# Layer norms moved into the attention passes, a four-bank score ring in the last group, and router logits with the router as weights

## The reference

```python
def attn(c, Wq, Wk, Wv):                     # 16 heads of 16
    Q, K, V = (c @ W reshaped to heads)
    alpha = softmax(Q K^T / sqrt(16))        # over all 1024 keys
    alpha = where(causal, alpha, 0)          # masked after the softmax
    return alpha V
def ffn(x, router_w, w_fc, w_proj):          # 8 experts, hidden 1024
    probs = softmax(x @ router_w)            # top 2, weights made to sum to 1
    return sum_e combine[e] * (gelu(x @ w_fc[e]) @ w_proj[e])
x = x + layernorm(attn(layernorm(x)))
x = x + layernorm(ffn(layernorm(x)))
```

## Time and profile before

| | us |
|---|---|
| median of 3 runs (1714.86 to 1717.33) | 1716.28 |
| time of the profiled execution | 1713.16 |
| its span, as the trace has it | 1711.4 |
| PE busy | 1520.0 (89%) |
| DVE busy | 970.5 (57%) |
| ACT busy | 813.6 (48%) |
| POOL busy | 607.4 (35%) |

### The profile page before, as it was taken

The page is one execution under the profiler, slowest core; times in us unless marked ns, Lnnn a source line. Parts: engine busy times, 40 slices in busy tenths (PEclk is TensorE's granted clock), DMA queues, the critical chain, the costliest instruction groups (busy, mean ns, idle before and its releaser), DMA issues.

```text
span 1711.4 us, 30057 instructions
## 1 busy us (share of the span) xinstructions
PE 1520.0 (89%) x8598; PEld 762.7 (45%) x8599; DVE 970.5 (57%) x1716; ACT 813.6 (48%) x1713; POOL 607.4 (35%) x700
## 2 busy tenths in 40 slices
PE   5988999998999899899999854599999999999990
PEld 3541333333333333233333333366767767667660
DVE  5769777777777677777777776422222222222224
ACT  2330777776777677677777720222222222222224
POOL 5332434344434344343444320033333333333322
PEclk9995999999999999999999975699999999999995
DMA  3579022220222211222202142622122122122129
GB/s 123 178 167 258 1 38 38 38 39 2 38 38 38 39 22 17 39 38 38 39 1 84 65 179 68 206 34 37 31 31 36 31 33 34 31 35 33 31 28 200
DMA packets 87631, 105.09 MB, mean 61 GB/s; under 512 B 11648, under 2 KB 70912, under 8 KB 87520
## 3 DMA queue, kind: packets, MB, share of 16 engines
q1 hardware_dynamic: 69664, 80.80, 20.1%
q0 software_dynamic: 17856, 22.89, 8.5%
HBM read 64.70 MB, written 38.96 MB: 61 GB/s over the span
## 4 chain that ended last, share of the span: by engine, by line
PE 70%; issue 11%; DVE 7%; ACT 5%; POOL 4%; DMA 1%; SPq 0%; DVEq 0%; POOLq 0%; ACTq 0%
PE ps L1059 14%; PE ps L1079 14%; PE ps L934 12%; PE ps L906 10%; PE ps L999 9%; PE ps L1069 4%; ACT wfc L799 3%; DVE negmax L1321 3%; PE ps L899 2%; POOL x L616 2%; PE ps L954 1%; PE ps L1050 1%; PE ps L986 1%; ACT wfc L840 1%; PE ps L946 1%
## 5 line engine op out<-in xcount | busy, mean ns | idle before, releaser
L1321 DVE TENSOR_REDUCE negmax<-ps 128x1 f32<-128x1024 f32 x512 | 603.0, 1219 | 167.3 <-PE ps L999 164.5
L799 ACT ACTIVATE wfc<-ps 128x512 f32<-128x512 f32 x768 | 436.7, 595 | 181.2 <-PE ps L906 172.2
L1059 PE MATMUL ps<-wfc,yx 128*128 x568 | 257.5, 596 | 1.3 <-DVE yx L1433 0.7
L1079 PE MATMUL ps<-arena,yx 128*128 x1136 | 257.0, 379 | 0.4 <-ACT yx L824 0.4
L677 POOL TENSOR_TENSOR wfc<-wfc,causal 128x512 f32<-128x512 f32 x128 | 163.1, 1274 | 252.9 <-ACT wfc L799 203.3
L699 POOL DMA_INDIRECT expert_out<-yx,rt x71 | 112.6, 1586 | 366.2 <-DVE yx L1446 366.2
L999 PE MATMUL ps<-arena 96*128 96x512 bf16 x704 | 231.4, 413 | 9.4 <-DVE negmax L1321 4.1
L906 PE MATMUL ps<-arena 120*128 120x512 bf16 x528 | 206.4, 395 | 17.9 <-ACT wfc L799 4.2
L1079 PEld LDWEIGHTS ps<-arena,yx 128*128 128x128 f32 x1136 | 210.4, 190 | 26.8 <-issue 1.1
L821 ACT ACTIVATE yx<-ps 128x512 f32<-128x512 f32 x142 | 84.8, 597 | 206.0 <-PE ps L1059 206.0
L934 PE MATMUL ps<-wfc 128*16 128x128 f32 (+4 forms) x2304 | 161.8, 383 | 0.0
(11 more groups left out here) (169 smaller groups left out, 1491.3 us busy)
## 6 DMA issues: line engine op xcount, KB each, us to landing
arena<-qk_parts SPq DMA_DIRECT2D x132, 128.0 KB, 5.6
qk_parts<-x SPq DMA_DIRECT2D x32, 384.0 KB, 2.6
arena<-in_L_ffn_w_proj SPq DMA_DIRECT2D x8, 1024.0 KB, 10.6
wfc<-in_L_ffn_w_fc SPq DMA_DIRECT2D x16, 512.0 KB, 7.4
wfc<-qk_parts SPq DMA_DIRECT2D x60, 128.0 KB, 6.2
expert_out<-rt SPq DMA_DIRECT2D x3, 1408.0 KB, 13.1
yx<-in_L_attn_content SPq DMA_DIRECT2D x8, 512.0 KB, 3.9
x<-in_L_attn_content SPq DMA_DIRECT2D x1, 4096.0 KB, 25.2
```

Source lines behind the costliest of these rows:

```text
L799: nc.scalar.activation(et_sb[b % NET][:, hl, :], bk(ebank(c)), ACT.Exp).then_inc(s_expB, 1)
L1059: ins = nc.tensor.matmul(bk(1 + hf), xsT[:, kc, :], wfc[:, ds(off + (kc * FF + hf * 512), 512)], start=(kc == 0), stop=(kc == KC - 1))
L1079: ins = nc.tensor.matmul(bk(5 + s)[:, 0:D], hidT[:, c, :], arena[:, ds(off + c * D, D)], start=(c == 0), stop=(c == FC - 1))
L1321: nc.vector.tensor_reduce(negmax[:, hl % 2, i:i + 1], ps[:, 2 * (k % 2):2 * (k % 2) + 2, :], AX.XY, ALU.max, negate=True).then_inc(s_max, 1)
```

## The change

- Six passes (0 to 5) are written out and passes 6 to 14 are a loop of three turns.
- In each of passes 6 to 15 DVE does both norms of two tiles, one step after the maximum of a slot (`STEADY`), with POOL's roots in slots 10 and 21. These are tiles 0 to 19. Tiles 20 to 31 stay in groups of four (`FOURS`), two in the drain and one after it.
- The last group's chunks go through banks 4, 5, 1 and 2 and wait for the chunk four before.
- The router takes the eight groups in the order 0 to 5, 7, 6, six of them in the drain, one every six slots. Transposes and copies go through bank 0 one after the other. The logits are 8 matmuls of 128 columns with the router as weights (padded to 32 columns), in four column strips; ACT copies them (`copy_l`) and one matmul with the identity turns them back (`turn_back`) into bank 3, which DVE clears.
- `lo1` moves into `yx`, over rows that SP has stored: `place(i)` waits for the store of its group. `w_proj` 6 and 7 are loaded before attention ends, 4 and 5 after the permutation and after the first two gathers.

```diff
@@ ring and plan @@
-        def ebank(c):
+        LAST_RING = (4, 5, 1, 2)
+        def ebank(c, g):
+            if isinstance(g, int) and g == NGR - 1:
+                return LAST_RING[c % 4]
             return 4 + c % 2
...
-        LN_STEP, TAIL_END = 8, 49
-        at_stats = [LN_STEP * g + 1 for g in range(G)]
...
+        ORDER = (0, 1, 2, 3, 4, 5, 7, 6)
+        FIRST_LN, NPAIR = 6, NGR - 6
+        FOURS = (5, 7, 6)
+        IN_TAIL = 6
+        STEADY = {7: ("bn_y", 0), 8: ("bn_y", 1), 9: ("var_y", 0), 13: ("add", 0), 17: ("add", 1),
+                  18: ("bn_x", 0), 19: ("bn_x", 1), 20: ("var_x", 0), 24: ("scale", 0), 26: ("scale", 1)}
+        ROOT_Y, ROOT_X = 10, 21
+        at_bn_y, at_var_y, at_root_y, at_add = (0, 38), (1, 39), (1, 39), (3, 41)
+        at_bn_x, at_var_x, at_root_x, at_scale = (4, 42), (5, 44), (5, 44), (7, 46)
+        at_first = [1 + 6 * i for i in range(IN_TAIL)]
+        at_turn_x = [x + 2 * kc for x in at_first for kc in range(KC)]
+        at_logits = [x + 4 for x in at_first]
+        at_copy_l = [x + 5 for x in at_first]
+        at_back = [x + 6 for x in at_first]
+        at_choose = [x + 8 for x in at_first]
+        at_count = [x + 10 for x in at_first]
+        at_place = [x + 11 for x in at_first]
...
-            for p in range(NSL):
-                body(p, p)
-            with eng.Fori(0, (NGR - 1 - NSL) // NSL) as r:
+            for p in range(2 * NSL):
+                body(p, p % NSL)
+            with eng.Fori(0, (NGR - 1 - 2 * NSL) // NSL) as r:
@@ SP @@
+            for i in range(4):
+                store_x2(i)
             sp.wait_ge(s_ST, NCH * (NGR - 2))
+            for e in (6, 7):
+                load_wproj(e)
             sp.wait_ge(s_vc, NGR)
             for e in range(4):
                 load_wproj(e)
+            store_x2(4)
             sp.wait_ge(s_ST, NCH * (NGR - 1))
             for c in range(6 * KC, 8 * KC):
                 load_wfc(c)
+            store_x2(5)
             sp.wait_ge(s_pv, NBU * NGR)
             for c in range(4 * KC):
                 load_wfc(c)
             sp.wait_ge(s_T4, 2 * NGR)
             for c in range(4 * KC, 6 * KC):
                 load_wfc(c)
+            for i in range(6):
+                store_gate(i)
+            for i in range(6, G):
+                store_x2(i)
+            for i in range(6, G):
+                store_gate(i)
             sp.wait_ge(s_inv, NPR // PCE)
-            for e in range(4, E):
+            for s in range(2):
+                sp.wait_ge(s_xs[s], 16)
+            for e in (4, 5):
                 load_wproj(e)
@@ POOL @@
+                    if ln_live(p) and k == ROOT_Y:
+                        root_y(p - FIRST_LN, 2)
+                    if ln_live(p) and k == ROOT_X:
+                        root_x(p - FIRST_LN, 2)
@@ ACT @@
+            def copy_x2(i, kc):
+                act.wait_ge(s_x2t, KC * i + kc + 1)
+                nc.scalar.copy(x2T[:, kc, :], bk(x_bank(i, kc))).then_inc(s_x2e, 1)
+            def copy_l(i):
...
+                act.wait_ge(s_lt, i + 1)
+                nc.scalar.copy(lgT[:, :], bk(0)[:, 0:P]).then_inc(s_lc, 1)
@@ PE @@
-                wait_pos(pe, s_expB, NCH * g + c - 1)
+                if isinstance(g, int) and g == NGR - 1 and c >= 2:
+                    pe.wait_ge(*((s_max, QT * NH) if c < 4 else (s_expB, NCH * g + c - 3)))
+                else:
+                    wait_pos(pe, s_expB, NCH * g + c - 1)
...
-                        ins = nc.tensor.matmul(bk(2)[:, (g * TPC + t) * E:(g * TPC + t + 1) * E],
-                                               x2T[:, kc, t * P:(t + 1) * P], router[:, kc, :],
-                                               start=(kc == 0), stop=(kc == KC - 1))
+                        ins = nc.tensor.matmul(bk(0)[32 * t:32 * t + 32, 0:P], router[:, kc, :], x2T[:, kc, t * P:(t + 1) * P],
+                                               start=(kc == 0), stop=(kc == KC - 1), skip_group_check=True)
+                ins.then_inc(s_lt, 1)
+            def turn_back(i):
...
+                if i:
+                    pe.wait_ge(s_rp, CRP * (i - 1) + 1)
+                pe.wait_ge(s_lc, i + 1)
+                nc.tensor.matmul(bk(bank)[:, c0:c0 + TE], lgT[:, :], ...
@@ DVE @@
+                dve.wait_ge(s_x2w[i], 16)
                 dve.wait_ge(s_lo, 3 * i + 3)
                 for j in range(TOPK):
-                    ins = nc.vector.tensor_tensor(lo1[:, j, tiles, :], ...
+                    ins = nc.vector.tensor_tensor(lo1[:, g, j, :, :], ...
...
+                    if isinstance(p, int) and p == NGR and k == 0:
+                        dve.wait_ge(s_max, QT * NH)
+                        nc.vector.memset(bk(3), 0.0).then_inc(s_bz, 1)
...
+                    if ln_live(p) and k in STEADY:
+                        steady(p, k)
...
+            dve.wait_ge(s_const, NCONST)
             groups(dve, body)
-            for g in range(in_tail(at_stats), G + 2):
-                if g <= G:
-                    ln_first(g)
-                ln_second(g)
+            four_bn_y(2)
+            var_y(four_c0(2), TPC)
+            four_add(2)
+            four_bn_x(2)
+            var_x(four_c0(2), TPC)
+            choose(6)
+            four_scale(2)
+            place(6)
+            choose(7)
```

More of the change, by code:

```diff
@@ L975, in body @@
                         count(g)
[L976 to L979 removed]
+                    for n in tail(at_turn_x, p, k):
+                        turn_x(*divmod(n, KC))
+                    for i in tail(at_logits, p, k):
+                        logits(i)
+                    for i in tail(at_back, p, k):
+                        turn_back(i)
                     for j, back in due(at_turn, k):
@@ L1289, in ln_second, with tile @@
[L1289 to L1308 removed]
+            def tile(buf, t):
+                return buf[:, ds(t, 1), :]
@@ new lines, in var_x, with add @@
+            def var_x(c0, n):
+                dve.wait_ge(s_bnx, c0 + n)
+                nc.vector.memset(pause[:, :], 0.0)
+                for j in range(n):
+                    nc.vector.bn_aggr(mv[:, 1, j, :], stats[:, 1, j, :]).then_inc(s_bnx, 1)
+                dve.wait_ge(s_bnx, c0 + 2 * n)
+                nc.vector.tensor_scalar(mv[:, 1, 0:n, 1], mv[:, 1, 0:n, 1], EPS, None, ALU.add).then_inc(s_varx, 1)
+            def add(t, j):
+                return nc.vector.scalar_tensor_tensor(out=tile(x1, t), in0=tile(yx, t), scalar=rstd[:, 0, j:j + 1],
+                                                      in1=tile(x1, t), op0=ALU.mult, op1=ALU.add)
@@ new lines, in keep_shift, with scale, steady @@
+            def keep_shift(t, n):
+                nc.vector.tensor_tensor(shift[:, ds(t, n)], mv[:, 0, 0:n, 0], rstd[:, 0, 0:n], ALU.mult).then_inc(s_shift, 1)
+            def scale(t, j):
+                return nc.vector.tensor_scalar(tile(yx, t), tile(x1, t), mv[:, 1, j, 0:1], rstd[:, 1, j:j + 1],
+                                               ALU.subtract, ALU.mult)
+            def steady(p, k):
+                step, j = STEADY[k]
+                m = p - FIRST_LN
+                t0 = 2 * m
+                if step == "bn_y":
+                    if j == 0:
+                        dve.wait_ge(s_norm, 2 * p - 4)
+                        nc.vector.memset(pause[:, :], 0.0)
+                    bn_y(t0 + j, j)
+                elif step == "var_y":
+                    var_y(4 * m, 2)
+                elif step == "add":
+                    if j == 0:
+                        dve.wait_ge(s_xin, 16)
+                        dve.wait_ge(s_rsy, m + 1)
+                        add(t0, 0)
+                    else:
+                        add(t0 + 1, 1).then_inc(s_add, 1)
+                        keep_shift(t0, 2)
+                elif step == "bn_x":
+                    if j == 0:
+                        dve.wait_ge(s_add, m + 1)
+                        nc.vector.memset(pause[:, :], 0.0)
+                    bn_x(t0 + j, j)
+                elif step == "var_x":
+                    var_x(4 * m, 2)
+                elif j == 0:
+                    dve.wait_ge(s_rsx, m + 1)
+                    scale(t0, 0)
+                else:
+                    scale(t0 + 1, 1).then_inc(s_x2, 1)
```

341 lines of the change are left out of this document (173 added, 168 removed).

## The result

The changed kernel takes 1674.38 us (median of 4 runs, 1669.85 to 1675.18), the kernel before 1715.57 us beside it (4 runs, 1712.78 to 1717.33): ratio 0.9756, 95% interval 0.9734 to 0.9778. It is faster by 2.4%. The forecast was 1672 us. The profiled executions have spans of 1711.4 and 1672.5 us, 38.9 us apart.

The account below looks back on a forecast made before the run. Bound: a tight chain over PE, ACT and DVE in passes, then router rounds one after another. Span 1711.4 - 4.9 + 10 - 11 - 35 - 3 = 1667.5, plus 1.8 and 3.1: 1672 us; 8-in-10 range 1652 to 1697.

Parts of the forecast that it names:

- One loop turn less: Attention loop: three turns instead of four save one branch back, -4.9 us, bounds -4 to -6.
- Norm steps: Ten passes with DVE's norms of two tiles: 1.0 us a pass, 10 us in all, bounds 1 to 28.
- the collision in slot 9: In a pass, DVE's epsilon add waits for POOL's L657: 1.1 us more, of which about 0.6 reaches PE.
- The drain: Stretch up to the last product with V, then 75.9 us: -11 us, bounds -17 and -3.
- the short logits: Drain: router logits as eight matmuls in strips, shorter in four rounds, -2 us.
- the early norms: Drain: five of eight groups normed before it, removing PE's waits for DVE, -5.5 us.
- the ring: Drain: four banks instead of two win about a quarter of ACT's 23.3 us of waits, 6 us.
- To the last `place`: Last product with V to the end of `place`: -35 us, including a 4.6 us store wait; bounds -40 and -29.
- To the second tile: Permutation to second expert tile: first gather wins 4 us, late load costs 1; -3 us, bounds -5 and +2.
- I give back 1 us: Before the second expert tile: 1 us lost because the `w_proj` load, 2 MB, lands late.
- The rival of collisions: Passes: two or three more POOL waits make 3 to 4 us a pass, 1692 to 1702 us; chance 0.15.
- The free drain: Drain: four banks win most of ACT's 23.3 us, store lands early, 12 to 18 us less; chance 0.12.

Follow-up runs that it names:

- e1: Kernel before with only the loop edit: passes 0 to 5 written out, three turns instead of four, no norms in passes; 1710.5 us, ratio 0.9967.
- e7: Changed kernel with the first epsilon add of a pass moved from slot 9 to 10 and its root from 10 to 11; 1673.6 us, ratio 0.9755.
- e8: Changed kernel with a pass's norm steps moved to where DVE has gaps or POOL is idle; 1686.7 us, ratio 0.9826.
- e6: Changed kernel with the last group's chunks back on banks 4 and 5 in turn, waiting for the exponential two back; 1675.8 us, ratio 0.9772.
- e4: Changed kernel with the last two groups' row stores put ahead of the six gate stores on SP; 1670.2 us, ratio 0.9740.
- e5: Changed kernel with the last two groups' row stores issued by ACT on its own queue; 1670.5 us, ratio 0.9742.
- e12: Changed kernel with six gate stores and both row stores ahead of the twelve `w_fc` loads, the last two gates behind; 1671.2 us, ratio 0.9740.
- e3: Changed kernel without SP's waits for the first two gathers ahead of the last two `w_proj` loads; 1675.0 us, ratio 0.9763.

## Why the forecast came out

**The total: near by luck in part.** The terms of the forecast make -43.9 us; the two spans differ by -38.9, so the sum missed by 5.0 us (1667.5 against 1672.5). The forecast then added 3.1 us because the profiled execution of the kernel before lay that far below its median. The changed kernel's profiled execution lies at its median (1674.25 and 1674.38), so this addition took back most of the miss, and 1672 came within 2.4 us of 1674.4. Within the terms, too, errors of opposite sign cancelled, as the next paragraphs show.

**One loop turn less, -4.9 us: right, and short by one part.** e1 gives -5.7 by the clock, -6.7 in the trace: the branch, and 0.4 us for each of three passes that leave the loop. The forecast saw no cost in written-out passes; it missed that they are quicker. In the changed kernel the two dearer branches (5.8 us) take about 2 us back.

**Norm steps, +1.0 us a pass: right in size, measured 0.9 in the loop and 0.73 without it; its parts were not.** The working gave 0.6 us to the collision in slot 9 and the rest mostly to slots 17 to 20. e7 gives 0.22 to the collision. The table of maxima gives 0.39 to the first add, for which the forecast had nothing but a share of 0.4 in the crowding after it, and 0.62 to slots 18 to 20, all of it given back by slot 24. The lock that the Trainium skill describes ("SBUF — State Buffer", section "SBUF: two separate sides") is confirmed in form by the lines above for POOL's multiply by `dmask` and its masks: the blocked step ends within 0.3 us of POOL's. It is not confirmed for POOL's root, beside which adds ran at 0.48 us. What a collision costs depends on the place: 0.22 of 1.21 us in slot 9; in e8 the norm steps of a pass take 2.0 us longer than in e7, and the pass grows by 1.3.

**The drain, -11 us: measured -10.8, again by other parts.** Of that four banks are 1.8 (forecast 6) and the short logits 3.6 (forecast 2), if what each loses when it alone is taken out may be added. The other 5.4 would then belong to the early norms less two router rounds (forecast 5.5 - 2.2); no run separates those two. That the total fits is luck: 4.2 us too much for the ring, 1.6 and 2.1 too little for the others. The step that failed is the quarter of ACT's 23.3 us of waits that the forecast gave the ring: with two banks in the changed drain (e6) ACT waits 12.0 us, with four 10.0, so 11.3 of the 23.3 go without the ring. The floor given as a bound is mis-subtracted as well: 54 us are -22, not -20.

**To the last `place`, -35 us: measured -32.7.** The new wait came where it was forecast, in `place(6)`, at 3.8 us for a forecast 4.6. But all of it lies later: the final norm ends at E + 9 instead of E + 5, the front of `place` is done at E + 20.3 instead of E + 16.4, and the store lands at E + 24 instead of E + 21, since the six stores of gates between loads and rows were left out of the working. With the gates moved behind it (e4) it landed at E + 21, as forecast. The bound of -40 without the wait does not come either: with the wait gone (e5, e12) the stretch takes 29.8 us, -34.4, because the logits of the last round, which the forecast had done by about E + 20, are there only at E + 24.

**To the second tile, -3 us: measured +0.9, and no gain in any case.** Kernels with the same code here spread from 21.0 to 25.3 us, around the 22.0 and 21.8 of the kernel before and e1, so the sign is not resolved. The gather did win what was said (PE gets its tile 3.7 us sooner after the permutation). "I give back 1 us" for `w_proj` is the part that failed: it was issued 7 us after the permutation's last product, as forecast, but was in at 16.2 us instead of 15 and needed at 13.0 instead of 14 to 15, and PE waited 3.3 us. PE's timeline of the changed kernel:
```profile
1063.44 1.09 PE L1161 MATMUL ps<-ident,yx 128*128 128x128 f32 x8 [3.26 <-DMA arena<-in_L_ffn_w_proj]
1064.74 5.39 PE L1151 MATMUL ps<-wfc,yx 128*128 x8 [0.20 <-issue]
```
The product behind the wait took 5.39 us at a granted clock of 0.69 (1064.7 to 1070.2), against 3.69 us at 1.00 in the kernel before, where PE had stood 0.6 us ahead of it and not 3.3. e3 shows the wait to move, not to go. The forecast's own bound of +2 covers this case.

The rival of collisions (3 to 4 us a pass) did not come, though e8 shows how near it lies: norm steps moved by a few slots bring 1.3 us of it. The free drain did not come either: ACT still waits 10 us for PE.

## What to carry to other kernels

A step added to a tight chain costs its length where the chain's instructions stand back to back, and is given back only at the chain's next wait. Look for those waits, and lay beside each candidate slot what POOL does then: here two gaps of DVE (slots 16 and 29) were just where POOL began. A store on which something waits belongs ahead of bulk loads in its queue, and a store's small size does not help behind them: six of 4 KB held SP for 10.0 us here, and five of 512 KB in the same place of the kernel before for 13.5. Gating one transfer on another only moved the wait here, since both were needed soon after. And a loop's branch that costs 5 us is worth writing out.

What a forecast should keep apart: a wait counted under one name (ACT's 23.3 us for chunks) may have several causes, and only a run with one of them taken out prices it; and a sum that comes out within its range can do so because its terms miss in opposite directions.

## What was not expected of the hardware

- A written-out pass is 0.4 us quicker than the same pass in the loop (50.24 against 50.64 us; with the norms 0.6, 50.97 against 51.55), and nine more written-out passes show no cost of fetching. The trace has register instructions in a pass of the loop (112 on PE, 79 on ACT, 48 on POOL and 53 on DVE in pass 7 of the changed kernel) and none on these engines in a written-out one; that they make the difference is likely but not shown.
- The branch back costs 4.8 to 5.1 us with the small body and mostly 5.8 with the norms in it; four of the 20 such steps in the looped kernels with norms were shorter, down to 3.5. Why is open.
- Six stores of 4 KB took SP 10.0 us to issue behind twelve loads of 512 KB, 4.9 us of it for one of them.
- The first gather is late with 2 MB of `w_proj` loads ahead of it (e3) as with 4 MB (before): the first tile's transposes start 9.3 and 9.5 us after the permutation's last product, 5.8 in the changed kernel. The stores to `out` follow these loads in both, so no run shows how much of it is the loads' doing.
